# One exponential a unit, the diagonal of maxima on GpSimd, outputs turned behind the scores, and ten unread matmuls in slots without expert tiles

## The chip, the cores and the metric

The kernel runs on one core of a Trainium2 chip. The metric is the device time of one execution in microseconds, median of the runs shown.

## What is computed

A decoder layer on 64 sequences of 64 tokens with 128 channels, in float32: causal self-attention with 16 heads of 8 channels, attention to a context of the same size, and a mixture of eight experts of which each token takes two, with a layer norm behind each.

```
a = softmax(q k / sqrt(8));  o = (a v) wo + bo            # twice: causal, then to ctx
x = layernorm(x + o) * g + b                              # after each
top2 of softmax(x rw + rb), their weights by softmax
out = sum over the two of  gelu(x w1[e] + b1[e]) w2[e] + b2[e]
x = layernorm(x + out) * g + b
```

Products whose result feeds a choice of experts are made of a high and a low float16 part of each factor, so that they keep nearly float32 accuracy.

## The kernel before

The program is written out by hand for each engine, as a list of *slots*; semaphores order the engines against each other. Four slots make a step, in which one block of 256 tokens passes self-attention and an earlier one cross-attention. A *unit* is half a block (two sequences, 128 tokens) in one of the two attentions; unit g starts in slot g, and there are 64 of them in slots 0 to 71. In slot g the engines work on different stages of several units:

- TensorE: turns the normalised attention output `o_n` of unit g-3 (`turn_o`, L1549) and the normalised row of unit g-5 (`turn_y`, L1562); makes the transposed scores of unit g-1 (`scores_T`: the diagonal of maxima first, L1513, the mask, L1518, then the products, L1525); the scores of unit g (`scores`, L1495 and L1501); where the slot has an expert tile, its first product (`up`); then `weigh` of unit g-2 (probabilities times values, L1541), `out_proj` of unit g-3 (L1557), the tile's second product (`down`, L1628), and projections.
- VectorE: low halves of projections, `norm` of unit g-4 (L1136), `maxima` of unit g (the row maxima from PSUM, L1089, then a product with a constant that puts them on diagonals, L1094, so that a matmul of ones subtracts them in the transposed scores), `probs_low` of unit g-1 for ten heads (L1082), the reciprocals and `o_n` of unit g-2 (L1103, L1108), residual and statistics of unit g-3 (L1122 to L1127), and routing.
- ScalarE: copies of turned outputs, then for unit g-1 two exponentials of the same 1024 columns of PSUM, `probT` in float32 (L889) and its high part `p_hi` in float16 (L892), then copies and Gelu for tiles, and high halves.
- GpSimd: `gain` of unit g-4 (L750, L756), scatters of rows to experts and gathers of their results (in some slots), `probs_low` of unit g-1 for the other six heads (L776), `spread` of unit g-3 (variance to inverse deviation, L762, L764), `x2_low` (L770).

`weigh` waits for both low parts. `scores_T` waits for the diagonal. `norm` waits for `spread`.

Slots 0 to 32 have no expert tile. Slots 33 to 76 have one or two, the rest of the tiles and the last block (through all experts) follow as a tail. In slots 8 to 15 ScalarE and VectorE also split one expert's first weights into halves (VectorE's part is L1352). Banks of PSUM are named by their use: the diagonal goes into two banks KEYS, expert results into bank H_B.

Of the kernel before, what the change touches and what calls it, by code (L numbers as in the profile page):

```python
# [6 lines left out]
B, S, D, H, FF, E = 64, 64, 128, 16, 512, 8  # L7
# [16 lines left out]
W1_SLOT = 8  # L24
CLEAR_SLOT, CLEAR_EVERY = 10, 2
DVE_HEADS = 10
# [198 lines left out]
def tiles_in(slot):  # L225
    return [Tile(m) for m in range(NMOE) if TILE_SLOT[m] == slot]

# [83 lines left out]
def build(nc, x, ctx_in, cst, w, out):  # L311
# [17 lines left out]
    with st:  # L329
# [162 lines left out]
        lo_first, lo_second = two("probs_lo_first_heads"), two("probs_lo_second_heads")  # L492
# [217 lines left out]
        def _(pool):  # L710
# [61 lines left out]
            def probs_low(u):  # L772

                pool.wait_ge(exp_done[u.kind], u.count())
                h = slice(DVE_HEADS, H)
                pool.tensor_tensor(p_lo[u.buf][:, h, :], probT[u.buf][:, h, :], p_hi[u.buf][:, h, :], ALU.subtract).then_inc(  # L776
                    lo_second[u.kind], 1)
# [43 lines left out]
            def slot(g):  # L821
# [15 lines left out]
                if u := unit_at(g - 1):  # L837
                    probs_low(u)
# [14 lines left out]
        def _(act):  # L853
# [29 lines left out]
            def exps(u, v):  # L883
# [3 lines left out]
                if v:  # L887
# [3 lines left out]
                               scale=float(HD) ** -0.5)  # L891
                act.activation(p_hi[u.buf][:, :, :].rearrange("p h q -> p (h q)"),  # L892
                               bank[:, KEYS:KEYS + 2, :].rearrange("p a n -> p (a n)"), ACT.Exp,
# [9 lines left out]
            def y_turned(u):  # L903
# [9 lines left out]
                if b.back(1).exists():  # L913
                    act.wait_ge(lg_ready, Unit(CROSS, b.back(1), u.pair).count())
                act.activation(x2_tile[u.buf][:, :], turned_y, ACT.Identity,
                               bias=ln_bc[a][:, :], scale=ln_gc[a][:, :]).then_inc(yT_done[a], 1)

# [52 lines left out]
            def slot(g):  # L970
# [14 lines left out]
                if u := unit_at(g - 5):  # L985
                    act.wait_ge(yT_ready[u.kind], u.count())
                if u := unit_at(g - 3):
                    o_turned(u, same_buffers(g - 3))
                if u := unit_at(g - 5):
                    y_turned(u)  # L990
                if (c := chunk_closes(g)) is not None:
                    copy_y(Tile(FIRST_TILE[c] + TILES_OF[c] - 1))
                if u := unit_at(g - 1):
                    exps(u, same_buffers(g - 1))
                for x in tiles[:1]:
                    tile_step(x)
# [46 lines left out]
        def _(dve):  # L1043
# [34 lines left out]
            def probs_low(u):  # L1078
# [712 lines left out]
```

## Time and profile before

| | us |
|---|---|
| median of 3 runs | 798.61 (795.01 to 799.62) |
| the profiled execution | 803.89 |
| its span, first to last instruction | 802.1 |
| busy: TensorE, VectorE, ScalarE, GpSimd | 596.7, 488.9, 453.3, 370.1 |
| mean granted share of TensorE's clock | 0.876 |

Busy times don't say what bounds a stage: each engine is idle in some of them. A granted share of 1 is 2.4 GHz, a share of 0.5 is 1.2 GHz; what lies between is a mean over both levels.

### The profile page before, as it was taken

The numbers are of one execution on the slowest core, as the hardware profiler recorded it, in microseconds if no ns is written. First come the engines' busy times: TensorE is split into PE (matmuls) and PEld (weight loads), VectorE is DVE, ScalarE is ACT, GpSimd is POOL, SyncE is SP. The second block draws the span as 40 slices with busy tenths as digits, with TensorE's granted clock in tenths as the row PEclk, the third lists the DMA queues.
The fourth block names the chain that finished last, engine by engine and source line by source line (L and its number), as shares of the span: only waits on it lengthen the run. The fifth ranks groups of instructions, "written<-read, shape, count | busy, mean of one in ns | idle before, by whom it ended". The sixth has DMA issues, their size and how long they took to land. (4 is left out here: it accounts for less than half of the span.)

```text
span 802.1 us, 21265 instructions
## 1 busy us (share of the span) xinstructions
PE 596.7 (74%) x7870; PEld 471.7 (59%) x7870; DVE 488.9 (61%) x1337; ACT 453.3 (57%) x824; POOL 370.1 (46%) x576
## 2 busy tenths in 40 slices
PE   2776676776767698887987988698777776878970
PEld 1344444545444476765766776476666666777870
DVE  3465879767696877888776578866334651221153
ACT  1223545444333589977997889688467554334320
POOL 7122243433337544435753665387237476530350
PEclk9965878877757999998999999899989888899995
DMA  4351554843132645544655675546546457778730
GB/s 111 106 174 54 161 170 128 287 125 87 34 93 66 198 146 168 164 130 139 195 155 177 185 205 171 151 140 174 162 142 191 141 176 222 234 239 266 234 96 20
DMA packets 141413, 124.64 MB, mean 155 GB/s; under 512 B 12224, under 2 KB 123600, under 8 KB 141312
## 3 DMA queue, kind: packets, MB, share of 16 engines
q1 hardware_dynamic: 134496, 113.06, 46.6%
q0 software_dynamic: 4368, 9.05, 4.1%
q8 instruction: 64, 1.05, 0.5%
q10 hardware_dynamic: 2448, 1.18, 0.5%
q14 instruction: 37, 0.30, 0.1%
HBM read 86.81 MB, written 38.54 MB: 156 GB/s over the span
## 5 line engine op out<-in xcount | busy, mean ns | idle before, releaser
L1089 DVE TENSOR_REDUCE row_max<-bank 128x16 bf16<-128x1024 f32 x64 | 78.3, 1224 | 79.4 <-PE bank L1501 78.6
L776 POOL TENSOR_TENSOR prob_lo<-probT,prob_hi 128x384 f16<-128x384 f32 x64 | 68.7, 1073 | 92.8 <-ACT prob_hi L892 92.4
L1549 PE MATMUL bank<-consts,o_n 128*128 128x64 f32 x256 | 47.7, 316 | 81.2 <-DVE o_n L1108 71.6
L1628 PE MATMUL bank<-w_in,w_hl 128*128 128x128 f32 x704 | 106.3, 298 | 0.0
L1549 PEld LDWEIGHTS bank<-consts,o_n 128*128 128x128 f32 x256 | 39.3, 220 | 95.3 <-issue 71.0
L1628 PEld LDWEIGHTS bank<-w_in,w_hl 128*128 128x128 f32 x704 | 93.8, 207 | 0.4
L889 ACT ACTIVATE probT<-bank 128x1024 f32<-128x1024 f32 x64 | 65.6, 1024 | 46.2 <-PE bank L1525 45.8
L762 POOL TENSOR_TENSOR veps<-mv,eps 128x1 f32<-128x1 f32 x64 | 14.5, 226 | 140.3 <-DVE mv L1127 140.3
L799 POOL DMA_INDIRECT w_hl<-ys,pos x60 | 59.6, 994 | 40.5 <-DMA ys<-w_hl 23.5
L1614 PE MATMUL bank<-xT,w_in 128*128 128x128 f16 x1056 | 77.9, 226 | 0.0
L1082 DVE TENSOR_TENSOR prob_lo<-probT,prob_hi 128x640 f16<-128x640 f32 x64 | 62.3, 973 | 24.9 <-ACT prob_hi L892 24.8
L933 ACT ACTIVATE w_hl<-bank 128x512 f32<-128x512 f32 x88 | 52.6, 597 | 39.3 <-PE bank L1614 38.8
L785 POOL DMA_INDIRECT xs<-x_hl,pos x60 | 62.2, 1036 | 17.8 <-issue 17.8
L1614 PEld LDWEIGHTS bank<-xT,w_in 128*128 128x128 f16 x1056 | 67.0, 102 | 0.0
L1525 PEld LDWEIGHTS bank<-q_st,k_all 128*64 128x64 f16 x2048 | 44.5, 126 | 36.4 <-issue 36.4
L892 ACT ACTIVATE prob_hi<-bank 128x1024 f16<-128x1024 f32 x64 | 65.1, 1018 | 0.0
L901 ACT ACTIVATE oT<-bank 128x128 f32<-128x128 f32 x64 | 17.7, 277 | 75.9 <-PE bank L1562 61.4
L750 POOL TENSOR_TENSOR yg<-yn,ln_g 128x128 f32<-128x128 f32 x64 | 29.5, 460 | 66.3 <-DVE yn L1136 66.3
L1094 DVE TENSOR_TENSOR max_diag<-consts_bf,row_max 128x1024 bf16<-128x1024 bf16 x64 | 53.4, 834 | 2.2
L1513 PE MATMUL bank<-max_diag,consts_bf 128*128 128x512 bf16 x128 | 47.8, 460 | 7.5 <-DVE max_diag L1094 7.5
L933 ACT ACT_TABLE_LOAD x41 | 52.6, 1283 | 0.7
L1525 PE MATMUL bank<-q_st,k_all 128*64 128x64 f16 x2048 | 52.1, 212 | 0.0
(173 smaller groups left out, 1556.8 us busy)
## 6 DMA issues: line engine op xcount, KB each, us to landing
w_in<-w_scr SPq DMA_DIRECT2D x96, 512.0 KB, 3.7
q_scr<-q_hl SPq DMA_DIRECT2D x64, 128.0 KB
k_scr<-k_hl SPq DMA_DIRECT2D x64, 128.0 KB, 2.3
q_st<-q_scr SPq DMA_DIRECT2D x32, 256.0 KB, 3.9
k_all<-k_scr SPq DMA_DIRECT2D x128, 64.0 KB, 2.1
xs_tile<-xs SPq DMA_DIRECT2D x42, 128.0 KB
ys<-w_hl SPq DMA_DIRECT2D x42, 128.0 KB, 2.1
xs<-xs_tile SPq DMA_DIRECT2D x3, 1472.0 KB, 6.8
```

Of the source, the lines that this page charges most:

```text
L776: pool.tensor_tensor(p_lo[u.buf][:, h, :], probT[u.buf][:, h, :], p_hi[u.buf][:, h, :], ALU.subtract).then_inc(lo_second[u.kind], 1)
L785: pool.indirect_dma_start(xs[c], bass.IndirectOffsetOnAxis(pos[c][:, k, t:t + 1], 0), x2_hl[:, n, :], None).then_inc(scattered[c], 16)
L799: pool.indirect_dma_start(got[f % 2][:, t, k, :], None, ys[c], bass.IndirectOffsetOnAxis(pos[c][:, k, n:n + 1], 0)).then_inc(got_in[f % 2] ...
L889: act.activation(probT[u.buf][:, :, :].rearrange("p h q -> p (h q)"), bank[:, KEYS:KEYS + 2, :].rearrange("p a n -> p (a n)"), ACT.Exp, sc ...
L892: act.activation(p_hi[u.buf][:, :, :].rearrange("p h q -> p (h q)"), bank[:, KEYS:KEYS + 2, :].rearrange("p a n -> p (a n)"), ACT.Exp, sca ...
L933: act.activation(hid[x.par][:, :, :].rearrange("p c t -> p (c t)"), expert_h(x), ACT.Gelu, scale=1 / W1_SCALE).then_inc(h_done, 1)
L1082: dve.tensor_tensor(p_lo[u.buf][:, h, :], probT[u.buf][:, h, :], p_hi[u.buf][:, h, :], ALU.subtract).then_inc(lo_first[u.kind], 1)
L1089: dve.reduce_max(row_max[u.buf][:, :], bank[:, SC:SC + 2, :].rearrange("p a (h k) -> p (a h) k", k=S), AX.X).then_inc(max_done[a], 1)
L1525: last = pe.matmul(bank[64 * h:64 * h + 64, KEYS + n, 64 * hh:64 * hh + 64], k[:, gg, j, c:c + 64], q[:, gg, c:c + 64], start=False, stop= ...
L1549: last = pe.matmul(turned_o[:, 64 * b:64 * b + 64], o_n[u.buf][:, b, :, :, :].rearrange("p c a d -> p (c a d)"), consts[:, C_DELTA:C_TRI], ...
L1614: last = pe.matmul(v[:, c * P:(c + 1) * P], w1_t[x.wb][:, i, c * P:(c + 1) * P], xT[x.par][:, j * P:(j + 1) * P], start=False, stop=True, ...
L1628: last = pe.matmul(expert_y(x), hid[x.par][:, c, :], w2_t[x.wb][:, c, :], start=False, stop=c == FC - 1, skip_group_check=True)
```

## The change

1. *One exponential.* ScalarE makes `probT` alone. VectorE casts it to `p_hi` and subtracts for all 16 heads, in two instructions; GpSimd's share of the subtraction goes.
2. *The diagonal on GpSimd.* The product of maxima and constant, 1024 bfloat16 elements a partition, moves from VectorE to GpSimd, behind `gain` and ahead of the slot's scatters and gathers.
3. *Outputs turned behind the scores.* In slots up to 32, which have no tile, TensorE's `turn_o` and `turn_y` come after `scores_T` and `scores`, and ScalarE's copies of them after the exponential. Slots with a tile keep their order.
4. *Unread matmuls.* In slots 0 to 32 TensorE makes two times five matmuls of 512 columns from constants into bank H_B, which nothing reads there.

(`probs_low` stands twice in the old program; the first piece with it is GpSimd's, the second VectorE's. The last piece is TensorE's slot.)

```diff
+KEEP_BUSY = 5
-DVE_HEADS = 10
+def turns_late(slot):
+    return not tiles_in(slot) and chunk_closes(slot) is None and slot < ATTENTION_END
...
-            def probs_low(u):
-                pool.wait_ge(exp_done[u.kind], u.count())
-                h = slice(DVE_HEADS, H)
-                pool.tensor_tensor(p_lo[u.buf][:, h, :], probT[u.buf][:, h, :], p_hi[u.buf][:, h, :], ALU.subtract).then_inc(
-                    lo_second[u.kind], 1)
+            def spread_maxima(u):
+                pool.wait_ge(max_done[u.kind], u.count())
+                m = row_max[u.buf][:, :].rearrange("p (a c) -> p a c", c=2).unsqueeze(2).to_broadcast([P, HP, S, 2])
+                dl = neg_delta.rearrange("p (q c) -> p q c", c=2).unsqueeze(1).to_broadcast([P, HP, S, 2])
+                pool.tensor_tensor(max_diag[u.buf][:, :, :, :], dl, m, ALU.mult).then_inc(diag_ready[u.kind], 1)
...
                 if u := unit_at(g - 4):
                     gain(u)
+                if u := unit_at(g):
+                    spread_maxima(u)
                 for c, n, k in scatters_at(g):
                     scatter(c, n, k)
...
-                act.activation(p_hi[u.buf][:, :, :].rearrange("p h q -> p (h q)"),
-                               bank[:, KEYS:KEYS + 2, :].rearrange("p a n -> p (a n)"), ACT.Exp,
-                               scale=float(HD) ** -0.5).then_inc(exp_done[a], 1)
...
+            def probs_low(u, v):
                 dve.wait_ge(exp_done[u.kind], u.count())
-                h = slice(0, DVE_HEADS)
-                dve.tensor_tensor(p_lo[u.buf][:, h, :], probT[u.buf][:, h, :], p_hi[u.buf][:, h, :], ALU.subtract).then_inc(
-                    lo_first[u.kind], 1)
+                if v:
+                    dve.wait_ge(pv_ready[v.kind], v.count())
+                dve.tensor_copy(p_hi[u.buf][:, :, :], probT[u.buf][:, :, :]).then_inc(hi_done[u.kind], 1)
+                dve.wait_ge(hi_done[u.kind], u.count())
+                dve.tensor_tensor(p_lo[u.buf][:, :, :], probT[u.buf][:, :, :], p_hi[u.buf][:, :, :], ALU.subtract).then_inc(
+                    lo_done[u.kind], 1)
...
+            def keep_busy(g):
+                if 0 <= g < ATTENTION_END and not tiles_in(g):
+                    for _ in range(KEEP_BUSY):
+                        pe.matmul(bank[:, H_B, :], ones_bf, cbf[:, 0:512], start=True, stop=True, skip_group_check=True)
...
-                u, v = unit_at(g - 3), unit_at(g - 5)
-                if u or v:
-                    turn_free()
...
+                if not turns_late(g):
+                    turn_both(g)
                 if u := unit_at(g - 1):
                     scores_T(g, u)
                 if u := unit_at(g):
                     scores(g, u)
+                if turns_late(g):
+                    turn_both(g)
                 for x in tiles[:1]:
                     up(x)
+                keep_busy(g)
...
                     weigh(u)
                 if u := unit_at(g - 3):
                     out_proj(u)
+                keep_busy(g)
```

The next rows are from VectorE's list, from `norm` of one unit to `o_n` of another, before the change.

```order
L1136 TENSOR_SCALAR yn<-res,mv,rstd 128x128
L1089 TENSOR_REDUCE row_max<-bank 128x16
L1094 TENSOR_TENSOR max_diag<-consts_bf,row_max 128x1024
L1082 TENSOR_TENSOR prob_lo<-probT,prob_hi 128x640
L1103 RECIPROCAL rden<-bank 64x16 x2
L1108 TENSOR_TENSOR o_n<-bank,rden 64x8x2x8 x2
```

The same stretch of VectorE's list after it.

```order
L1143 TENSOR_SCALAR yn<-res,mv,rstd 128x128
L1100 TENSOR_REDUCE row_max<-bank 128x16
L1091 CAST prob_hi<-probT 128x1024
L1093 TENSOR_TENSOR prob_lo<-probT,prob_hi 128x1024
L1110 RECIPROCAL rden<-bank 64x16 x2
L1115 TENSOR_TENSOR o_n<-bank,rden 64x8x2x8 x2
```

The diagonal has gone from behind the maximum, and a cast and a subtraction of all 1024 elements stand there. On GpSimd, the rows of one slot before were these.

```order
L750 TENSOR_TENSOR yg<-yn,ln_g 128x128
L756 TENSOR_TENSOR x_rows<-yg,b_bo 128x128
L776 TENSOR_TENSOR prob_lo<-probT,prob_hi 128x384
L762 TENSOR_TENSOR veps<-mv,eps 128x1
L764 TENSOR_TENSOR rstd<-veps,minus_half 128x1
```

And these are GpSimd's rows of such a slot now.

```order
L755 TENSOR_TENSOR yg<-yn,ln_g 128x128
L761 TENSOR_TENSOR x_rows<-yg,b_bo 128x128
L782 TENSOR_TENSOR max_diag<-consts_bf,row_max 128x1024
L767 TENSOR_TENSOR veps<-mv,eps 128x1
L769 TENSOR_TENSOR rstd<-veps,minus_half 128x1
```

The place of the subtraction is taken by the diagonal. TensorE's list, in a slot without a tile, had the turning first.

```order
L1549 MATMUL bank<-consts,o_n 128x64 x2
L1562 MATMUL bank<-consts,yn 128x128
L1513 MATMUL bank<-max_diag,consts_bf 128x512 x2
L1518 MATMUL bank<-consts_bf 128x512 x2
L1525 MATMUL bank<-q_st,k_all 64x64 x32
L1501 MATMUL bank<-k_all,q_st 64x256 x8
```

Now TensorE's list has it behind the scores, with five unread matmuls (L1653) after it.

```order
L1520 MATMUL bank<-max_diag,consts_bf 128x512 x2
L1525 MATMUL bank<-consts_bf 128x512 x2
L1532 MATMUL bank<-q_st,k_all 64x64 x32
L1502 MATMUL bank<-consts_bf 128x512 x2
L1508 MATMUL bank<-k_all,q_st 64x256 x8
L1555 MATMUL bank<-consts,o_n 128x64 x2
L1568 MATMUL bank<-consts,yn 128x128
L1653 MATMUL bank<-consts_bf 128x512 x5
```

The wait for `o_n` no longer stands ahead of the scores there.

## Rows read from the trace of the kernel before

**Rows 1.** Windows, of the maximum (L1089) alone: its busy time and count, granted clock, DMA
```profile
75.00:203.50 128.50, 19.58 (x16) 0.79 0.51 153
203.50:283.00 79.50, 11.02 (x9) 0.78 0.34 100
283.00:443.00 160.00, 23.27 (x19) 0.96 0.55 161
443.00:570.00 127.00, 14.66 (x12) 0.97 0.57 168
```

**Rows 2.** Waits from 75 to 283 us: total, times, longest
```profile
PE bank L1549 <- DVE o_n L1108: 54.1, 23, 3.3
...
DVE row_max L1089 <- PE bank L1501: 35.1, 18, 3.9
```

**Rows 3.** Windows, all engines: PE, PEld, DVE, ACT, POOL busy (count), clock, DMA
```profile
75.00:203.50 128.50, 91.59 (x1224) 62.13 (x1226) 97.74 (x221) 59.58 (x112) 44.85 (x81) 0.79 0.51 153
...
283.00:443.00 160.00, 137.94 (x2105) 109.87 (x2104) 122.16 (x317) 138.82 (x235) 79.96 (x128) 0.96 0.55 161
```

**Rows 4.** Timeline of a slot with a tile: start, length, instruction, idle before
```profile
315.37 1.23 DVE L1089 TENSOR_REDUCE row_max<-bank 128x16 bf16<-128x1024 f32 x1 [1.53 <-PE bank L1501]
...
316.63 0.69 DVE L1094 TENSOR_TENSOR max_diag<-consts_bf,row_max 128x1024 bf16<-128x1024 bf16 x1
...
316.72 1.38 POOL L776 TENSOR_TENSOR prob_lo<-probT,prob_hi 128x384 f16<-128x384 f32 x1 [1.81 <-ACT prob_hi L892]
...
317.24 1.54 DVE L1082 TENSOR_TENSOR prob_lo<-probT,prob_hi 128x640 f16<-128x640 f32 x1
...
319.25 0.59 DVE L1108 TENSOR_TENSOR o_n<-bank,rden 64x128 f32<-64x128 f32 x2
...
319.99 0.63 PE L1549 MATMUL bank<-consts,o_n 128*128 128x64 f32 x4 [0.76 <-DVE o_n L1108]
...
320.57 0.61 PE L1513 MATMUL bank<-max_diag,consts_bf 128*128 128x512 bf16 x2
...
321.02 0.59 PE L1518 MATMUL bank<-consts_bf 128*128 128x512 bf16 x2
...
322.02 0.73 POOL L743 TENSOR_TENSOR x_bo<-tok_in,bo 128x256 f32<-128x256 f32 x1
...
322.07 0.61 PE L1501 MATMUL bank<-k_all,q_st 128*64 128x256 f16 x8
...
322.72 1.23 DVE L1089 TENSOR_REDUCE row_max<-bank 128x16 bf16<-128x1024 f32 x1 [0.58 <-PE bank L1501]
...
324.68 0.82 DVE L1082 TENSOR_TENSOR prob_lo<-probT,prob_hi 128x640 f16<-128x640 f32 x1
```

**Rows 5.** Timeline of VectorE, a slot without tiles
```profile
152.74 1.23 DVE L1089 TENSOR_REDUCE row_max<-bank 128x16 bf16<-128x1024 f32 x1 [0.57 <-PE bank L1501]
...
154.61 1.53 DVE L1082 TENSOR_TENSOR prob_lo<-probT,prob_hi 128x640 f16<-128x640 f32 x1
156.07 0.51 DVE L1103 RECIPROCAL rden<-bank 64x16 f32<-64x16 f32 x2
...
159.68 1.23 DVE L1089 TENSOR_REDUCE row_max<-bank 128x16 bf16<-128x1024 f32 x1
```

**Rows 6.** Timeline, GpSimd ahead of VectorE
```profile
224.56 0.91 POOL L776 TENSOR_TENSOR prob_lo<-probT,prob_hi 128x384 f16<-128x384 f32 x1
224.71 1.32 DVE L1094 TENSOR_TENSOR max_diag<-consts_bf,row_max 128x1024 bf16<-128x1024 bf16 x1
```

**Rows 7.** Groups of instructions: second exponential, smallest subtraction on GpSimd
```profile
L892 ACT ACTIVATE prob_hi<-bank 128x1024 f16<-128x1024 f32 x64 | 65.1, 1018 | 0.0
...
L770 POOL TENSOR_TENSOR x_hl<-x_rows,x_hl 128x128 f16<-128x128 f32 x32 | 13.5, 423 | 0.0
```

**Rows 8.** Groups of instructions: low part of expert weights, one scatter
```profile
L785 POOL DMA_INDIRECT xs<-x_hl,pos x60 | 62.2, 1036 | 17.8 <-issue 17.8
...
L1352 DVE SCALAR_TENSOR_TENSOR w_hl<-w_in,w_hl 128x512 f16<-128x512 f32 x8 | 5.4, 673 | 0.1
```

More of the change, by code:

```diff
@@ L491, in build @@
         v_hi_ready = two("v_hi_ready")
-        lo_first, lo_second = two("probs_lo_first_heads"), two("probs_lo_second_heads")
+        hi_done, lo_done = two("probs_hi"), two("probs_lo")
         lg_ready, lg_done, route = sem("lg_ready"), sem("lg_done"), sem("route_step")
@@ L836, in slot @@
                     last_spread(f)
-                if u := unit_at(g - 1):
-                    probs_low(u)
                 if u := unit_at(g - 3):
@@ L890, in exps @@
                                bank[:, KEYS:KEYS + 2, :].rearrange("p a n -> p (a n)"), ACT.Exp,
-                               scale=float(HD) ** -0.5)
-                act.activation(p_hi[u.buf][:, :, :].rearrange("p h q -> p (h q)"),
-                               bank[:, KEYS:KEYS + 2, :].rearrange("p a n -> p (a n)"), ACT.Exp,
                                scale=float(HD) ** -0.5).then_inc(exp_done[a], 1)
@@ L916, in y_turned, with both_turned @@
                                bias=ln_bc[a][:, :], scale=ln_gc[a][:, :]).then_inc(yT_done[a], 1)
+            def both_turned(g):
+                if u := unit_at(g - 5):
+                    act.wait_ge(yT_ready[u.kind], u.count())
+                if u := unit_at(g - 3):
+                    o_turned(u, same_buffers(g - 3))
+                if u := unit_at(g - 5):
+                    y_turned(u)
             def x2_high(u):
@@ L984, in slot @@
                     act.wait_ge(late_in, 16 * LATE_WEIGHTS)
[L985 to L990, printed above, removed]
+                if not turns_late(g):
+                    both_turned(g)
                 if (c := chunk_closes(g)) is not None:
@@ L994, in slot @@
                     exps(u, same_buffers(g - 1))
+                if turns_late(g):
+                    both_turned(g)
                 for x in tiles[:1]:
@@ L1090, in maxima @@
                                bank[:, SC:SC + 2, :].rearrange("p a (h k) -> p (a h) k", k=S), AX.X).then_inc(max_done[a], 1)
-                dve.wait_ge(max_done[a], u.count())
-                m = row_max[u.buf][:, :].rearrange("p (a c) -> p a c", c=2).unsqueeze(2).to_broadcast([P, HP, S, 2])
-                dl = neg_delta.rearrange("p (q c) -> p q c", c=2).unsqueeze(1).to_broadcast([P, HP, S, 2])
-                dve.tensor_tensor(max_diag[u.buf][:, :, :, :], dl, m, ALU.mult).then_inc(diag_ready[a], 1)
             def outputs(u):
@@ L1359, in slot @@
                 if u := unit_at(g - 1):
-                    probs_low(u)
+                    probs_low(u, same_buffers(g - 1))
                 if u := unit_at(g - 2):
@@ L1532, in weigh @@
                 a, b = u.kind, u.blk
-                pe.wait_ge(lo_first[a], u.count())
-                pe.wait_ge(lo_second[a], u.count())
+                pe.wait_ge(lo_done[a], u.count())
                 pe.wait_ge(v_done[a], b.times(1, 1))
@@ L1563, in turn_y, with turn_both @@
                 turned.append((yT_done[u.kind], u.count()))
+            def turn_both(g):
+                u, v = unit_at(g - 3), unit_at(g - 5)
+                if u or v:
+                    turn_free()
+                if u:
+                    turn_o(u)
+                if v:
+                    turn_y(v)
             def logits(u):
@@ L1682, in slot @@
                     pe.wait_ge(late_in, 16 * LATE_WEIGHTS)
-                u, v = unit_at(g - 3), unit_at(g - 5)
-                if u or v:
-                    turn_free()
-                if u:
-                    turn_o(u)
-                if v:
-                    turn_y(v)
+                if not turns_late(g):
+                    turn_both(g)
                 if (c := chunk_closes(g)) is not None:
@@ L1695, in slot @@
                     scores(g, u)
+                if turns_late(g):
+                    turn_both(g)
                 for x in tiles[:1]:
```

1 line of the change is left out of this document (removed).

## The prediction

> **What bounds the kernel now.** I read first how many units of attention (one row maximum each) end in which stretch, with the granted clock, then the chain of waits, then single slots of the timeline. Of the 64 units, 25 end between 75 and 283 us, in slots without expert tiles: 16 in 128.5 us (8.03 us each), then 9 in 79.5 us (8.83). 19 end from 283 to 443 us beside one expert tile a slot (8.42), 12 from 443 to 570 us (10.6) [rows 1]; the last four end among tail tiles. What follows them (the rest of the tail, the dense experts) is not edited.
>
> In the slots without tiles the longest waits of the two engines that matter point at each other: TensorE waits 54.1 us for `o_n` before it turns it, VectorE waits 35.1 us for the scores before the maximum [rows 2]. So the period is one loop: maximum, diagonal, low part, reciprocals, `o_n` on VectorE, then turning, `scores_T`, `scores` on TensorE. TensorE is busy 91.6 of 128.5 us at a mean granted clock of 0.79, a mix of 2.4 and 1.2 GHz [rows 3].
>
> One slot with a tile shows the same loop closed: the maximum starts at 315.37, runs 1.23, the diagonal 0.69 from 316.63, the low part of ten heads ends at 318.78, `o_n` at 319.84, TensorE turns from 319.99, starts `scores_T` at 320.57, ends `scores` at 322.68, and the next maximum starts at 322.72: 7.35 us [rows 4]. VectorE alone has a loop of its own in a slot without tiles where the scores come early: from the maximum at 152.74 to the next at 159.68, 6.94 us, with 3.61 of it from the reciprocals at 156.07 on (outputs, residual, statistics, the two small powers on GpSimd, norm) [rows 5].
>
> **A lock that both loops hit.** In [rows 4] GpSimd's `prob_lo` starts at 316.72, while VectorE's diagonal runs to 317.32, and takes 1.38; VectorE's `prob_lo`, issued at 317.24, takes 1.54. Alone the two take 0.91 and 0.82 [rows 4, 6]. GpSimd got nothing until 317.32, ended 0.78 later at 318.10, and only then VectorE did its work, ending 0.68 later. The other way round in [rows 6]: GpSimd's 0.91 from 224.56 is undisturbed, and the diagonal that starts 0.15 later takes 1.32 in place of 0.69, ending 0.56 after it. So a GpSimd product and a VectorE instruction of these kinds exclude each other for a whole instruction, and the one that waits goes next. The Trainium skill (SBUF — State Buffer, "SBUF: two separate sides") calls the shared port pair "an exclusive lock, not a bandwidth split" and counts a VectorE operation in a two-port mode, a float32 copy too, among those that take it. By that rule, the trace agrees for the two-input kinds; no row here shows the copy.
>
> **The change, part by part.**
>
> *ScalarE* loses 64 exponentials of 1.02 us [rows 7]. From 283 to 443 us it is busy 138.8 of 160 us, 7.3 a unit [rows 3], so in some of those slots it is the limit, in others VectorE is, as in [rows 4]. The edit takes that limit to 6.3 and shortens nothing that VectorE closes.
>
> *VectorE* loses the diagonal (0.69 alone) and its 640 elements (0.82), and gains a cast of 1024 elements and a subtraction of 1024. The trace has no such cast: the cheapest row of its size is the 16-bit diagonal, 0.69, the dearest the maximum, 1.23 for as many elements [rows 4]. I take 0.69, since it is SBUF to SBUF with one input. For the subtraction I take the rate of the maximum, 1.23: 640 in 0.82 continues to it.
>
> *GpSimd* loses 384 elements and gains the diagonal of 1024, right behind the maximum. Its price D is the largest unknown. Rows for sums and differences: 128 elements 0.42, 256 in 0.73, 384 in 0.91 [rows 4, 6, 7]. From 128 to 384 that is 1.91 ns an element and gives 0.42 + 896 x 0.00191 = 2.13; from 128 to 256, 2.4 ns and 2.6 us. I take 2.25, nearer the first, whose rows write 16 bits too. Bounds: 0.69, if it ran as on VectorE, and 3.4, eight times the row of 128. The Trainium skill (GPSIMD Engine Reference, "Elementwise — side-by-side cycle accounting") has about 2.6 cycles an element at 1.2 GHz for two inputs, which as an estimate is 2.2 us for the elements and 2.4 with a start; the sum would be some 7 us longer by it.
>
> *The order.* At the end of the maximum both the cast (VectorE, in 0.03) and the diagonal (GpSimd, semaphore about 0.1) are ready. The cast goes first and ends at 0.72. GpSimd, waiting, is next, and ends at 0.72 + D - 0.13 = 2.84 (in [rows 4] it took 0.78 of its 0.91 after it was let in). The subtraction then ends 1.23 - 0.14 = 1.09 later, at 3.93. Before, the low part ended 318.78 - 316.60 = 2.18 after the maximum in [rows 4], 2.17 in [rows 5]. So the stretch from maximum to low part grows by **1.75 us** in each unit whose loop VectorE closes. The diagonal has left VectorE's list but not its time.
>
> *Slots with a tile* keep their old order on TensorE, so the loop stays: 7.35 + 1.75 = 9.1 us.
>
> *Slots without a tile* turn outputs behind the scores, which breaks the loop through TensorE. What is left is VectorE's own, 6.94 + 1.76 = 8.7 us. TensorE's, from the maximum over the product to `scores_T` and `scores`, is 1.27 + 2.84 + 0.06 + 2.7 = 6.9, and hides. The ten matmuls cost 0.225 each at full clock (two take 0.45, 320.57 to 321.02 [rows 4]), 2.2 us; TensorE's 91.6/16 = 5.7 busy us a unit [rows 3] and these make 7.9, still under 8.7, and lift the busy share from 0.71 to 0.9. The slots with tiles, that busy, are granted 0.96 [rows 1], so I take the clock near 1. Its gain lies under VectorE's loop and is worth nothing here.
>
> *Sum.* 75 to 203 us: 16 units at 8.7, eight of them with 0.67 more for the low part of the first expert weights [rows 8], which VectorE no longer hides: 144.6 - 128.5 = +16. 203 to 283 us: three units of routing, on VectorE already, +1.75 each; four with three scatters each, 1.04 us a piece [rows 8], which now stand behind the product on GpSimd and hold the power for the next norm to about 9.4, +1; two at 8.7: together +12. 283 to 443 us: 19 units, +1.75 where VectorE closed the loop and less where ScalarE did, 1.5 on the mean: +28. 443 to 570 us: 10.6 us a unit, where a second tile or four gathers often bound: +1 each, +12. The first four and the last four units +3. Total **+71 us**. The profiled execution is 803.9 us (span 802.1), 5.3 over the median of 798.6; 798.6 + 71 gives **870 us**.
>
> **The rivals.**
> 1. *GpSimd's product costs much less, or VectorE's work goes beside it* (ends faster). If the exclusion does not hold for the cast and the 16-bit product, or the subtraction gets in first, the low part ends 1.9 after the maximum, the product at 3.9, and `scores_T` starts at once: slots with a tile 3.9 + 0.06 + 2.13 + 0.04 + 1.23 = 7.4, slots without about 7.7 by the two engines' own loops: 25 x -0.5 and 31 x -0.1, **about 783 us**. The same if D is 0.7. For it: nothing in the rows, but no row has this product. Against: [rows 4, 6]. It decides below D = 2.25 - 71/60, about 1.1 us. Chance 0.09.
> 2. *Break even*, D near 1.1 or half of the stalls hidden where ScalarE bound: within 4 us of **799 us**. Chance 0.05.
> 3. *The clock stays low in the slots without tiles*, so that the unread matmuls are in the way: twice 0.225 each at 1.2 GHz, 4.5 a slot, beside 5.7 x 0.79/0.5 = 9.0 of the rest, 13.5 us against 8.7: 25 x 4.8 more, **990 us**. Against: the busy share rises. Chance 0.02.
> 4. *D near its upper bound*, 3.4 (the broadcast operands read slowly): 60 x 1.15 = 69 more, **939 us**. Chance 0.05.
> 5. The forecast, D between 1.9 and 2.7: 60 units x 0.35 or 0.45 either way is 849 to 897. Chance 0.79.
>
> **How the numbers follow.** The range takes the forecast's own bounds, some 11 us below for the stretches costed by a mean, and above them the part of rival 4 up to D = 3.0: 838 to 915. Outside stay rivals 1 to 3 and the rest of 4, 0.19. A difference under 0.5% (4 us) can't be told from none by this kernel's runs. Faster: rival 1 and a part of 2, 0.10. Same 0.04. Slower 0.86.
>
> **What would show it.** The diagonal on GpSimd lasting 2.8 or so when it waits behind the cast and 2.1 to 2.4 alone; VectorE's full subtraction at about 3 us in place of 1.2; VectorE busy (stalled) most of each slot from 75 to 283 us; the wait of TensorE for `o_n` gone there, but grown in slots with tiles; the granted clock near 1 from 75 us on; ScalarE some 64 us less busy; 25 units in about 236 us, 19 in about 188. It is wrong if the product lasts about 1 us, if the subtraction runs undisturbed beside it, or if the exponential comes so late that GpSimd's product is done before the cast wants to start.

## The result and the profile after

The changed kernel takes 866.17 us (median of 4 runs, 864.23 to 868.99) against 799.0 (795.01 to 799.62) for the kernel before on the same chip: a ratio of 1.0855, 95% interval 1.0808 to 1.0902. The profiled execution took 865.69 us, its span 863.9. The forecast was 870. What is said of single stretches comes from one profiled execution of each kernel, and these lie up to 9 us beside the median of their runs.

The page of the changed kernel, its span and busy times:

```profile
span 863.9 us, 21892 instructions
...
PE 655.3 (76%) x8200; PEld 496.7 (57%) x8200; DVE 585.6 (68%) x1337; ACT 400.0 (46%) x760; POOL 462.2 (54%) x576
```

ScalarE is 53 us less busy, not the 64 or so of the forecast: the exponential that went had overlapped its neighbours by about 0.1 us at either end. GpSimd is 92 us more busy, as moved work would make it. VectorE is 97 us *more* busy, although it lost a product and gained only a cast and 384 more elements a unit. Where that comes from, the groups of instructions of the page say (busy time and mean ns of one, then the idle time before them), and below them each line's shortest/median/longest duration in ns:

```profile
L782 POOL TENSOR_TENSOR max_diag<-consts_bf,row_max 128x1024 bf16<-128x1024 bf16 x64 | 144.0, 2249 | 74.3 <-DVE row_max L1100 72.5
...
L1093 DVE TENSOR_TENSOR prob_lo<-probT,prob_hi 128x1024 f16<-128x1024 f32 x64 | 164.1, 2563 | 2.2
...
L1091 DVE CAST prob_hi<-probT 128x1024 f16<-128x1024 f32 x64 | 46.0, 719 | 9.4 <-ACT probT L894 9.3
```

```profile
L782 POOL TENSOR_TENSOR max_diag<-consts_bf,row_max x64: 1892/2272/2873, 29.2 to 681.5; 128x1024 bf16<-128x1024 bf16 x64
L1093 DVE TENSOR_TENSOR prob_lo<-probT,prob_hi x64: 1224/2799/2801, 36.0 to 686.9; 128x1024 f16<-128x1024 f32 x64
L1091 DVE CAST prob_hi<-probT x64: 676/683/2302, 35.2 to 686.2; 128x1024 f16<-128x1024 f32 x64
```

A subtraction that can take 1.22 us takes 2.80 in 54 of 64 units. In the other ten it runs before the product or without one, and takes 1.2 to 1.4. Two slots of the timeline show why. First VectorE and GpSimd of the changed kernel in a slot without a tile (start, duration, engine):

```profile
149.66 1.21 DVE L1100 TENSOR_REDUCE row_max<-bank 128x16 bf16<-128x1024 f32 x1
150.79 0.68 DVE L1091 CAST prob_hi<-probT 128x1024 f16<-128x1024 f32 x1
...
151.51 2.80 DVE L1093 TENSOR_TENSOR prob_lo<-probT,prob_hi 128x1024 f16<-128x1024 f32 x1
154.23 0.51 DVE L1110 RECIPROCAL rden<-bank 64x16 f32<-64x16 f32 x2
...
157.69 1.23 DVE L1100 TENSOR_REDUCE row_max<-bank 128x16 bf16<-128x1024 f32 x1
```

```profile
150.95 2.27 POOL L782 TENSOR_TENSOR max_diag<-consts_bf,row_max 128x1024 bf16<-128x1024 bf16 x1
```

The product starts at 150.95, during the cast, which ends at 151.47; it ends at 153.22. The subtraction, issued at 151.51, ends at 154.31, 1.09 after the product. That is the order of the forecast: cast, product, subtraction, one at a time. And a slot with a tile, with TensorE's rows:

```profile
338.18 1.23 DVE L1100 TENSOR_REDUCE row_max<-bank 128x16 bf16<-128x1024 f32 x1 [2.60 <-PE bank L1508]
...
339.32 0.68 DVE L1091 CAST prob_hi<-probT 128x1024 f16<-128x1024 f32 x1
...
339.49 2.27 POOL L782 TENSOR_TENSOR max_diag<-consts_bf,row_max 128x1024 bf16<-128x1024 bf16 x1 [2.84 <-DVE row_max L1100]
...
340.04 2.80 DVE L1093 TENSOR_TENSOR prob_lo<-probT,prob_hi 128x1024 f16<-128x1024 f32 x1
...
343.31 0.59 DVE L1115 TENSOR_TENSOR o_n<-bank,rden 64x128 f32<-64x128 f32 x2
...
344.05 0.63 PE L1555 MATMUL bank<-consts,o_n 128*128 128x64 f32 x4 [1.97 <-DVE o_n L1115]
...
345.12 1.05 PE L1525 MATMUL bank<-consts_bf 128*128 128x512 bf16 x2
346.10 1.06 PE L1532 MATMUL bank<-q_st,k_all 128*64 128x64 f16 x32
346.98 1.04 PE L1508 MATMUL bank<-k_all,q_st 128*64 128x256 f16 x8
...
348.06 1.23 DVE L1100 TENSOR_REDUCE row_max<-bank 128x16 bf16<-128x1024 f32 x1 [1.86 <-PE bank L1508]
```

The loop of [rows 4] is still there, but longer: the low part ends 3.43 us after the maximum (342.84 less 339.41) where it was 2.18, TensorE stands idle 1.97 us for `o_n`, and the next maximum comes 9.88 us after this one (348.06 less 338.18), not 7.35. One thing is new: two matmuls of 512 columns need 0.98 us (345.12 to 346.10), where two of that size took 0.45 in [rows 4]. TensorE has come out of its wait at the lower of its two clock levels, 1.2 GHz.

The windows of the maximum alone, as in [rows 1] (stretch, length, busy time and count, granted clock, DMA share, GB/s):

```profile
75.50:208.50 133.00, 19.55 (x16) 0.92 0.50 148
208.50:299.50 91.00, 10.98 (x9) 0.88 0.32 97
299.50:491.50 192.00, 23.27 (x19) 0.87 0.44 130
491.50:637.00 145.50, 14.67 (x12) 0.89 0.49 146
```

Taken from one unit's maximum to another's, over whole groups of slots, the time went here:

| slots | before, us a unit | after | difference in all | forecast |
|---|---|---|---|---|
| 8 to 23 | 8.03 | 8.30 | +4 | +16 |
| 24 to 32 | 8.86 | 10.11 | +11 | +12 |
| 33 to 51 | 8.43 | 10.11 | +32 | +28 |
| 52 to 65 (12 units) | 10.51 | 12.09 | +19 | +12 |
| the first 8 and 66 to 71 | | | +3 | +3, with the last four units |
| behind the last maximum | 191.7 | 183.7 | -8 | 0 |

The chain of waits has moved with it. Of 76 to 299 us (waited for; total, times, longest):

```profile
PE bank L1520 <- POOL max_diag L782: 24.3, 16, 3.9
```

TensorE's 54.1 us for `o_n` in [rows 2] have gone there, and it waits for GpSimd's diagonal instead. In the slots with tiles, 299 to 491 us, `o_n` is its longest wait; before, from 283 to 443 us, the same wait came to 6.5 us in 6 units:

```profile
PE bank L1555 <- DVE o_n L1115: 37.8, 17, 5.2
```

### The profile page after: what moved, and what is told of

Read it like the earlier page. It is cut to its first block, busy times and chain, and to the rows that moved or that the text cites. A ratio compares the mean times of both kernels' runs of the same rounds, so it can differ in the third digit from the quotient of the medians.

```text
span 863.9 us, 21892 instructions
## 1 busy us (share of the span) xinstructions
PE 655.3 (76%) x8200; PEld 496.7 (57%) x8200; DVE 585.6 (68%) x1337; ACT 400.0 (46%) x760; POOL 462.2 (54%) x576
## 4 chain that ended last, share of the span: by engine, by line
issue 25%; PE 22%; DVE 21%; POOL 17%; DMA 4%; ACT 2%; SPq 1%; POOLq 0%; DVEq 0%; ACTq 0%
POOL xs L790 6%; PE bank L1643 4%; DVE prob_hi L1091 3%; DVE row_max L1100 3%; PE bank L1629 2%; DVE rden L1110 2%; POOL w_hl L804 2%; POOL max_diag L782 2%; PE bank L1532 2%; PE bank L1508 2%; PE bank L1555 2%; DVE o_n L1115 1%; PE bank L1520 1%; POOL rstd L769 1%; DMA q_scr<-q_hl 1%
## 5 line engine op out<-in xcount | busy, mean ns | idle before, releaser
L782 POOL TENSOR_TENSOR max_diag<-consts_bf,row_max 128x1024 bf16<-128x1024 bf16 x64 | 144.0, 2249 | 74.3 <-DVE row_max L1100 72.5
L1093 DVE TENSOR_TENSOR prob_lo<-probT,prob_hi 128x1024 f16<-128x1024 f32 x64 | 164.1, 2563 | 2.2
L1555 PE MATMUL bank<-consts,o_n 128*128 128x64 f32 x256 | 45.1, 303 | 76.1 <-DVE o_n L1115 71.0
L1643 PE MATMUL bank<-w_in,w_hl 128*128 128x128 f32 x704 | 102.2, 291 | 0.0
L1643 PEld LDWEIGHTS bank<-w_in,w_hl 128*128 128x128 f32 x704 | 89.8, 200 | 0.5
L1555 PEld LDWEIGHTS bank<-consts,o_n 128*128 128x128 f32 x256 | 36.9, 208 | 90.3 <-issue 78.5
L1653 PE MATMUL bank<-consts_bf 128*128 128x512 bf16 x330 | 85.8, 395 | 0.0
L804 POOL DMA_INDIRECT w_hl<-ys,pos x60 | 62.2, 1037 | 41.5 <-DMA ys<-w_hl 25.0
L790 POOL DMA_INDIRECT xs<-x_hl,pos x60 | 70.0, 1167 | 16.0 <-issue 16.0
L1143 DVE TENSOR_SCALAR yn<-res,mv,rstd 128x128 f32<-128x128 f32 x64 | 25.3, 395 | 54.1 <-POOL rstd L769 53.4
L903 ACT ACTIVATE oT<-bank 128x128 f32<-128x128 f32 x64 | 17.7, 277 | 91.3 <-PE bank L1568 83.1
```

The lines of the kernel that those rows point to most:

```text
L782: pool.tensor_tensor(max_diag[u.buf][:, :, :, :], dl, m, ALU.mult).then_inc(diag_ready[u.kind], 1)
L790: pool.indirect_dma_start(xs[c], bass.IndirectOffsetOnAxis(pos[c][:, k, t:t + 1], 0), x2_hl[:, n, :], None).then_inc(scattered[c], 16)
L804: pool.indirect_dma_start(got[f % 2][:, t, k, :], None, ys[c], bass.IndirectOffsetOnAxis(pos[c][:, k, n:n + 1], 0)).then_inc(got_in[f % 2] ...
L1093: dve.tensor_tensor(p_lo[u.buf][:, :, :], probT[u.buf][:, :, :], p_hi[u.buf][:, :, :], ALU.subtract).then_inc(lo_done[u.kind], 1)
L1555: last = pe.matmul(turned_o[:, 64 * b:64 * b + 64], o_n[u.buf][:, b, :, :, :].rearrange("p c a d -> p (c a d)"), consts[:, C_DELTA:C_TRI], ...
L1643: last = pe.matmul(expert_y(x), hid[x.par][:, c, :], w2_t[x.wb][:, c, :], start=False, stop=c == FC - 1, skip_group_check=True)
```

## The experiments

"Us a unit" are, in this order, slots 8 to 23, 24 to 32, 33 to 51 and 52 to 65. Ratios are to the kernel before on the same chip, with their 95% interval. Medians of runs on different chips are set side by side below; the kernel before took 798.02, 799.58 and 798.14 us on the three chips of these runs, and 799.0 on that of the first comparison.

### Which part costs: the changed kernel with one part undone

**Part 2 undone: the diagonal back on VectorE, behind the maximum.**

```diff
-                if u := unit_at(g):
-                    spread_maxima(u)
...
+                dve.wait_ge(max_done[a], u.count())
...
+                dve.tensor_tensor(max_diag[u.buf][:, :, :, :], dl, m, ALU.mult).then_inc(diag_ready[a], 1)
```

> The changed kernel with the diagonal back on VectorE behind the maximum; one exponential, late turns and unread matmuls stay. Exclusion theory: the stretch from the end of the maximum to the end of the low part falls from 3.43 us to 0.69 + 0.68 + 1.22 = 2.6, the low part runs 1.2 us undisturbed in nearly every unit, slots with a tile fall from 9.9 to about 8, slots without from 8.3 to about 7.9 (TensorE with its ten matmuls); 795 to 805 us. Rival (the cast and the full subtraction on VectorE, or the unread matmuls, are what costs): the time stays within 15 us of 866.

Measured: 796.61 us, ratio 0.9998 (0.9962 to 1.0035); 7.85, 8.64, 8.79 and 10.80 us a unit. The whole loss is gone. VectorE's group of the subtraction, and a slot of it:

```profile
L1091 DVE TENSOR_TENSOR prob_lo<-probT,prob_hi 128x1024 f16<-128x1024 f32 x64 | 78.5, 1227 | 2.2
```

```profile
315.79 1.23 DVE L1098 TENSOR_REDUCE row_max<-bank 128x16 bf16<-128x1024 f32 x1 [0.57 <-PE bank L1510]
317.05 0.69 DVE L1103 TENSOR_TENSOR max_diag<-consts_bf,row_max 128x1024 bf16<-128x1024 bf16 x1
317.65 0.69 DVE L1089 CAST prob_hi<-probT 128x1024 f16<-128x1024 f32 x1
318.38 1.23 DVE L1091 TENSOR_TENSOR prob_lo<-probT,prob_hi 128x1024 f16<-128x1024 f32 x1
```

Three instructions on VectorE end 2.59 us after the maximum, less than the 3.43 of two of them beside GpSimd's product. So the loss hangs on where the product is made. Whether by its length (rival: `scores_T` waits for it) or by the exclusion, this run doesn't tell; the next one does.

**The exclusion taken away, the product left on GpSimd.** In place of the subtraction from `probT`, VectorE takes the maximum of the scores in PSUM and `p_hi`, an instruction of the same size. The low parts are then not those of the probabilities; TensorE makes new scores only when VectorE has done with the old.

```diff
-                dve.tensor_tensor(p_lo[u.buf][:, :, :], probT[u.buf][:, :, :], p_hi[u.buf][:, :, :], ALU.subtract).then_inc(
+                dve.tensor_tensor(p_lo[u.buf][:, :, :], bank[:, SC:SC + 2, :].rearrange("p a (h q) -> p (a h) q", q=S), p_hi[u.buf][:, :, :], ALU.max).then_inc(
                     lo_done[u.kind], 1)
...
+                if v := next((v for q in range(g - 2, g - 9, -1) if (v := unit_at(q))), None):
+                    pe.wait_ge(lo_done[v.kind], v.count())
```

> The changed kernel, but the low part is not computed: the same VectorE instruction takes the larger of the scores in PSUM and the high part, so it reads one operand from SBUF, not two; outputs are therefore not the reference's. Its size and place stay, and the scores of a later unit wait for it. Exclusion theory: it no longer waits for GpSimd's product, lasts 1.2 us in place of 2.8, and ends about 2.0 us after the maximum in place of 3.43; slots with a tile fall from 9.9 to 7.5, about 800 us in all. Rival (the length of GpSimd's product itself, on the way to the transposed scores, is what costs, whoever else runs): within 15 us of 866.

Measured: 810.59 us, ratio 1.0145 (1.0105 to 1.0185); 8.06, 8.68, 8.73, 10.75 us a unit. From the page, and then one of the two units in which GpSimd was first:

```profile
L1093 DVE TENSOR_TENSOR prob_lo<-bank,prob_hi 128x1024 f16<-128x1024 f32 x64 | 78.4, 1225 | 2.2
```

```profile
331.62 1.90 POOL L782 TENSOR_TENSOR max_diag<-consts_bf,row_max 128x1024 bf16<-128x1024 bf16 x1 [0.27 <-DVE row_max L1100]
331.64 2.42 DVE L1091 CAST prob_hi<-probT 128x1024 f16<-128x1024 f32 x1
334.10 1.22 DVE L1093 TENSOR_TENSOR prob_lo<-bank,prob_hi 128x1024 f16<-128x1024 f32 x1
```

With one operand in PSUM the instruction never waits (1225 ns on the mean, 1.22 here), the product lasts as long as before, and 56 of the 70 us between the changed kernel and the last run (866.17 less 796.61) are back. So the exclusion between product and subtraction is the cause of most of it. The edit swaps subtraction for maximum too. That this is not what lets the instruction through shows in the kernel of part 2 alone, further down: there VectorE's two subtractions of `v_lo`, with one operand in PSUM as well, run inside a product of GpSimd in 0.86 us together, 0.42 on the mean of all 64.

```profile
28.53 1.89 POOL L784 TENSOR_TENSOR max_diag<-consts_bf,row_max 128x1024 bf16<-128x1024 bf16 x1 [6.78 <-DVE row_max L1098]
28.98 0.86 DVE L1083 TENSOR_TENSOR v_lo<-bank,v_hi 64x256 f16<-64x256 f32 x2 [0.54 <-ACT v_hi L889]
```

Some 14 us remain for the product's own length ahead of `scores_T`, for the cast (shut out in 2 of 64 units), and for a path that the run shows beside them: the product stands ahead of the small powers on GpSimd, and VectorE's `norm` waits for them 55.2 us here from 76 to 578 us, against 17.7 us from 72 to 572 with the product on VectorE.

```profile
DVE yn L1143 <- POOL rstd L769: 55.2, 32, 4.5
```

```profile
DVE yn L1145 <- POOL rstd L769: 17.7, 26, 2.0
```

The timeline rows above add what no row of before could show: a cast of float32 to float16 is shut out as well, for all of GpSimd's 1.90 us. The Trainium skill (SBUF — State Buffer, "SBUF: two separate sides") counts the float32 copy among the instructions that take the lock; by that rule, this trace agrees, with 2.42 us in place of 0.68.

**Part 4 undone: no unread matmuls** (`KEEP_BUSY = 0`).

> The changed kernel with no unread matmuls, all else as changed. Exclusion theory: VectorE's loop binds the slots without tiles, so the clock there falls from 0.92 to about 0.75 and the time moves little: 866 to 880 us. Rival (the unread matmuls stand in the way): 840 to 855 us.

Measured: 874.23 us, ratio 1.0935 (1.0879 to 1.0991); 8.20, 10.04, 10.34, 12.11 us a unit. The granted clock in slots 8 to 23, 0.92 with them, is 0.77:

```profile
79.00:210.30 131.30, 19.55 (x16) 0.77 0.50 149
```

There they raise the clock and gain nothing (8.20 against 8.30). The 8 us lie elsewhere. Three of them are in the first 8 slots, which have unread matmuls too: the maximum of slot 8 starts at 79.2 us without them and at 76.3 with them, at a granted clock of 0.80 and 1.00 up to there. Four lie in slots 33 to 51 and two behind the last maximum, where the edit changes no instruction, and their cause is open.

**Part 3 undone: the outputs turned ahead of the scores everywhere** (`turns_late` returns False).

> The changed kernel with outputs turned ahead of the scores in all slots, as before. Theory: the loop through o_n closes again in the slots without tiles, 1.27 + 3.4 + 1.06 + 0.15 + 2.7 = 8.6 us at full clock and up to 10.8 at half, against 8.3 now: 25 units x 0.3 to 2.5, 875 to 925 us. Rival (VectorE's own loop binds anyway, the order is worth nothing): within 5 us of 866.

Measured: 887.66 us, ratio 1.113 (1.1079 to 1.118); 9.19, 10.78, 10.21, 12.08 us a unit. The loop through TensorE is closed again in the first two groups: 0.89 a unit over 16 and 0.67 over 9 make 20 of the 21 us.

### What the low clock beside tiles costs

**Eight more unread matmuls in each slot with a tile**, at its end, where TensorE waited for `o_n`.

```diff
+                if tiles and g < ATTENTION_END and not tiles[-1].tail:
+                    pe.wait_ge(h_done, tiles[-1].m + 1)
+                    for _ in range(8):
+                        pe.matmul(bank[:, H_B, :], ones_bf, cbf[:, 0:512], start=True, stop=True, skip_group_check=True)
```

> The changed kernel with eight more unread matmuls of 512 columns at the end of TensorE's part of each slot with a tile, where it waits about 2 us for o_n. Theory: part of what slots with a tile lost (9.1 to 9.9 and more, where 8.6 follows from the longer stretch on VectorE) is TensorE's clock, granted 0.87 there in place of 0.96, since it waits longer; with the wait filled the clock rises to 0.95 or more and the slots fall by about 0.9 us, 838 to 850 us. Rival (the clock is no part of it; VectorE's stretch is all): within 5 us of 866, or above it by what the matmuls take.

Measured: 860.1 us, ratio 1.0777 (1.0733 to 1.082); 8.22, 10.10, 9.81, 12.10 us a unit. Windows of the maximum, slots with one tile:

```profile
298.50:484.50 186.00, 22.94 (x19) 0.97 0.47 137
```

The clock rose from 0.87 to 0.97 as meant, and 19 units gave back 0.3 us each: 6 us, where 16 to 28 were expected. In slots 52 to 65 it rose from 0.89 to 0.96 and gave back nothing. The expectation counted each half-clock matmul of the slot. Only those on the loop can count, between `o_n` and the next maximum; that most of the others lie where TensorE waits anyway is my reading, and no run takes them apart.

### The parts alone: the kernel before with one part added

**Part 2 alone: the diagonal on GpSimd, both exponentials kept.**

```diff
+            def spread_maxima(u):
+                pool.wait_ge(max_done[u.kind], u.count())
...
+                pool.tensor_tensor(max_diag[u.buf][:, :, :, :], dl, m, ALU.mult).then_inc(diag_ready[u.kind], 1)
...
+                if u := unit_at(g):
+                    spread_maxima(u)
...
-                dve.tensor_tensor(max_diag[u.buf][:, :, :, :], dl, m, ALU.mult).then_inc(diag_ready[a], 1)
```

> The kernel before with the diagonal alone moved to GpSimd, ahead of its share of the low part; two exponentials, low part split 10 to 6 heads, old order, no unread matmuls. Exclusion theory: VectorE's 640 elements and GpSimd's 1.89 us exclude each other; where GpSimd is first the low part ends 2.65 us after the maximum in place of 1.9 to 2.2, where VectorE is first it ends at 0.9 and the diagonal at 2.6: 805 to 835 us. Rival (the diagonal on GpSimd costs only together with the cast and the full subtraction): within 5 us of 798 or below.

Measured: 817.22 us, ratio 1.0262 (1.0209 to 1.0316); 7.45, 8.64, 8.83, 11.39 us a unit. Two groups, and a collision on VectorE:

```profile
L784 POOL TENSOR_TENSOR max_diag<-consts_bf,row_max 128x1024 bf16<-128x1024 bf16 x64 | 143.3, 2240 | 76.8 <-DVE row_max L1098 75.0
...
L1091 DVE TENSOR_TENSOR prob_lo<-probT,prob_hi 128x640 f16<-128x640 f32 x64 | 68.5, 1070 | 33.4 <-ACT prob_hi L901 33.2
```

```profile
302.50 1.81 DVE L1091 TENSOR_TENSOR prob_lo<-probT,prob_hi 128x640 f16<-128x640 f32 x1 [0.84 <-ACT prob_hi L901]
...
310.28 0.82 DVE L1091 TENSOR_TENSOR prob_lo<-probT,prob_hi 128x640 f16<-128x640 f32 x1
```

The same product of 2.2 us on GpSimd costs some 20 us here (18 by the medians, 21 by the ratio, from runs that lie between 808 and 824) and 70 in the changed kernel (796.61 to 866.17). VectorE has less beside it that can be shut out (640 elements, no cast), and in 48 of 64 units it isn't: its mean is 1.07 us against 0.82 undisturbed. A second path shows here as well. The product now stands ahead of the small powers on GpSimd's list, and VectorE's `norm` waits for these 90.4 us from 79 to 581 us, where before it waited 29.4 us from 75 to 570:

```profile
DVE yn L1141 <- POOL rstd L764: 90.4, 38, 6.5
```

So this run doesn't price the exclusion alone, and how its loss divides between the two paths isn't shown. The profiled execution is the fastest of the four, 9 us under their median. In it slots 8 to 23 gain 0.6 us a unit, 9 us in all, and the slots before them lose 4 and slots 52 to 65 lose 11.

**Parts 3 and 4 on the kernel before, and part 3 alone.** `turn_both` behind the scores in slots without tiles and ScalarE's copies behind the exponentials; the first of the two also with `keep_busy`.

```diff
-                u, v = unit_at(g - 3), unit_at(g - 5)
-                if u or v:
-                    turn_free()
...
+                if not turns_late(g):
+                    turn_both(g)
                 if u := unit_at(g - 1):
                     scores_T(g, u)
                 if u := unit_at(g):
                     scores(g, u)
+                if turns_late(g):
+                    turn_both(g)
```

> The kernel before with the late turns and the unread matmuls alone (parts 3 and 4); exponentials, diagonal and low part as before. Theory: the loop through o_n is gone in the slots without tiles, but ten matmuls fill TensorE, so they stay near 7.8 us as in the run with the diagonal on VectorE, against 8.03: 788 to 796 us. Rival (these parts are worth nothing): 798.

> The kernel before with the late turns alone (part 3). Theory: VectorE's own loop of about 7 us and TensorE's 5.7 busy us a unit bind the slots without tiles, 7.3 us in place of 8.03 and 8.86, so 25 units gain 0.6 to 1.0: 775 to 785 us, if the clock does not fall. Rival (the clock falls below 0.79 when nothing fills TensorE's waits, and takes the gain back): 790 us or more.

Measured: both parts 791.13 us, ratio 0.991 (0.9877 to 0.9943), 7.85, 8.15, 8.48, 10.52 us a unit; part 3 alone **781.45 us, ratio 0.9776 (0.9743 to 0.9809)**, 7.37, 8.31, 8.44, 10.52. Windows of the maximum, part 3 alone:

```profile
71.00:189.00 118.00, 19.57 (x16) 0.85 0.56 166
189.00:263.80 74.80, 10.99 (x9) 0.82 0.39 113
263.80:424.00 160.20, 23.27 (x19) 0.96 0.54 159
```

16 units in 118.0 us, not 128.5, and 9 in 74.8, not 79.5; the slots with tiles are untouched. This is the fastest version of all. The unread matmuls on top of it cost 10 us by the medians. In the profiled executions, 5 us apart, slots 8 to 23 lose 0.48 a unit with them: TensorE is busy 107.5 of 125.5 us there, against 85.6 of 118.0 without, and the clock goes from 0.85 to 0.93. Slots 24 to 32 gain 0.16.

**Parts 1 and 3, without the diagonal on GpSimd and without unread matmuls.**

> The kernel before with one exponential (cast and full subtraction on VectorE) and the late turns in slots without tiles; diagonal on VectorE, no unread matmuls. It differs from the run with late turns alone (781) by part 1 only. Theory: the end of the low part comes 2.6 us after the maximum in place of 1.9 to 2.2, on VectorE's path, and ScalarE's relief pays in a few slots with a tile only: 786 to 796 us. Rival (ScalarE bound the slots with a tile): below 778 us.

Measured: 795.39 us, ratio 0.9981 (0.9946 to 1.0016); 7.57, 8.64, 8.82, 10.80 us a unit. One exponential less on ScalarE, paid for by a cast and 384 elements on VectorE, costs 14 us against part 3 alone by the medians, 16 by the ratios.

### Late turns in the slots with tiles too

The edit is one condition, put on three kernels: the changed one, the kernel before with part 3, and the kernel with parts 1 and 3.

```diff
-    return not tiles_in(slot) and chunk_closes(slot) is None and slot < ATTENTION_END
+    return chunk_closes(slot) is None and slot < ATTENTION_END
```

> The changed kernel with the late turns in slots with a tile too (all but those that close a chunk). Loop theory: the longer stretch on VectorE costs there because TensorE turns o_n ahead of the scores; with that order gone VectorE's own loop of 8.2 us binds, slots with a tile fall from 10.1 to 8.5 to 9, and the kernel to 820 to 845 us. Rival (the stretch itself, or the product's place ahead of the transposed scores, binds in any order): within 5 us of 866.

> The kernel before with the late turns in all slots (all but those that close a chunk), no other part of the change. Theory: ScalarE, 7.3 us busy a unit, and TensorE with the tile bind the slots with a tile in the regular ones, so they gain at most 0.5 us each on the late turns' 781: 770 to 781 us. Rival (turned copies now delay the tile's turning and Gelu on ScalarE, which binds): 785 us or more.

> One exponential with the cast and full subtraction on VectorE, the diagonal on VectorE, late turns in all slots, no unread matmuls. Theory: with the turns late in slots with a tile, VectorE's own loop of 6.94 + 0.4 = 7.3 and ScalarE's 6.3 bind less than now: 760 to 778 us, the best of all. Rival (ScalarE was no limit, and the cast only lengthens VectorE's list): no better than the same order with two exponentials.

Measured: on the changed kernel 843.85 us, ratio 1.0548 (1.0498 to 1.0598), 8.23, 9.67, 9.32, 11.84 us a unit. On the kernel before with part 3, 830.16 us, ratio 1.0399 (1.0341 to 1.0457), 7.38, 7.93, 10.00, 11.73. With parts 1 and 3, 798.96 us, ratio 0.9988 (0.9956 to 1.002), 7.55, 8.30, 8.97, 11.11.

The first gains 22 us on the changed kernel. TensorE's wait for `o_n` beside tiles is 2.5 us there, not 37.8, and with no matmul added the granted clock in slots 33 to 51 is 0.94, not 0.87. The second loses 49 us on part 3 alone, 1.56 us a unit in slots 33 to 51, where a gain was expected. The third was expected to be the best of all (760 to 778) and is 4 us slower than the same kernel with early turns beside tiles. Of the second, the longest wait of a TensorE matmul from 285 to 440 us, and the place of it:

```profile
PE bank L1612 <- ACT x_tile L920: 18.9, 7, 3.0
```

```profile
318.28 1.02 ACT L894 ACTIVATE probT<-bank 128x1024 f32<-128x1024 f32 x1
...
319.20 1.02 ACT L897 ACTIVATE prob_hi<-bank 128x1024 f16<-128x1024 f32 x1
...
320.26 0.47 ACT L920 ACTIVATE x_tile<-bank,ln_bc,ln_gc 128x128 f32<-128x128 f32 x1
...
320.88 0.37 PE L1612 MATMUL bank<-ident_f,xs_tile 128*128 128x128 f16 x2 [2.87 <-ACT x_tile L920]
```

Turned late, `y` is copied out of its bank only behind two exponentials, and the tile's own turning, next on TensorE, waits 2.87 us for that copy. In a slot without a tile nothing stands there. With parts 1 and 3, and so one exponential, the waits for `x_tile` come to 12.5 us in 270 to 430 us, and with the stretched loop of the changed kernel there is more to gain from opening it. That this balance gives the one edit both signs is my reading; no run takes the two apart.

## Why the prediction was right

The step on which it rested stands. The forecast's order (cast, then the product that waited, then the subtraction) is seen in 54 of 64 units; GpSimd's product alone lasts 1.89 us and 2.27 behind a cast; VectorE's subtraction "at about 3 us" is 2.80. Undoing part 2 alone takes the loss away (1.0855 to 0.9998), and letting the last of the three read PSUM, with the product untouched, takes 56 of 70 us away. Rival 1, in which the work goes side by side, fell with the 2.80 us of L1093, and rivals 3 and 4 with a clock of 0.92 and a product of 1.89.

Its terms were less good than their sum, and that the sum came within 4 us is in part luck:

- **D, the product's price.** Taken at 2.25 us, it is 1.89 alone, the lower edge of "D between 1.9 and 2.7": the line through rows with float32 operands, from 128 to 384 elements, was too steep for this product. From the cast's end it takes 1.75, not 2.12, and the cast ends 0.60 after the maximum, not 0.72; the subtraction's 1.09 behind it is as forecast. So the low part ends 3.43 after the maximum and a unit's stretch grows by 1.25 us, not 1.75. At 1.25 us for 19 units the slots with one tile would have lost 24 us.
- **75 to 203 us, +16.** It was +4. The period forecast was 8.7 us and 0.67 for the expert weights; the usual slot there is 8.23 (8.03 in the one shown), which is 8.7 less the 0.5 by which the stretch was overrated. The 0.67 costs nothing: the slots that have it, 8 to 15, take 8.17 on the mean, and 16 to 23 take 8.44. VectorE does that work between the statistics and the norm, where it waits for the small powers on GpSimd: in one slot it starts at 114.37, lasts 0.66, and `norm` behind it still waits 0.71 us; before the change it was 107.46, 0.66 and 0.72.
- **203 to 283 us, +12.** It was +11. The terms that are named (three times 1.75, four times 1, two at 8.7 against a mean of 8.83) make 9, so the agreement is not theirs.
- **283 to 443 us, +28.** It was +32, by other terms: 1.25 a unit make 24; the clock, which fell from 0.96 to 0.87 because TensorE now waits about 2 us for `o_n` ahead of `scores_T`, makes some 6 by the run that filled the wait; 2 are open. That TensorE's waits beside tiles took the clock down has a second witness in the changed kernel with late turns everywhere: there the wait is gone and the clock is 0.94. The forecast let the clock near 1 everywhere and didn't ask what a longer wait does to it. That an edit which fills TensorE in one place starves it in another was the missed rival.
- **443 to 570 us, +12.** It was +19, 1.58 a unit where 1 was taken; there too `o_n` comes late in more slots than the mean of [rows 1] suggested: TensorE waits for it 23.0 us in 7 units, where it waited 5.6 us in 4. VectorE's `norm` waits 21.8 us for the small powers on GpSimd, where it waited 16.5. The clock is not the cause: filling the slots with matmuls took it from 0.89 to 0.96 and left the period at 12.10. How the 7 us more than forecast divide among the rest stays open.
- **The tail, 0.** It is 8 us shorter in the profiled execution. Nothing was edited there, it lay between 183 and 192 us in the profiled executions of the other kernels (183 to 189 with the product on GpSimd, 187 to 192 with it on VectorE), and its cause is open.

The errors cancel: 12 us too many in the first stretch and 8 in the tail against 11 too few beside tiles, so the span grew by 61.8, with 71 forecast. The median grew by 67 because the profiled execution of before lay 5 us over its median and that of the changed kernel did not: that, too, brings the forecast nearer to the result than its terms are. That the clock's gain from the unread matmuls "is worth nothing here" was right for slots 8 to 32 (8.20 without them, 8.30 with, in slots 8 to 23), as was the wait of TensorE for `o_n` gone there and grown beside tiles. "The granted clock near 1 from 75 us on" was wrong: 0.92, then 0.87 to 0.89.

The parts, priced by these runs: part 3 alone takes 18 us off the kernel before; part 1 on top of it adds 14 to 16; part 4 adds 10 on part 3 alone, nothing measurable with part 1 beside it (795.39 to 796.61), and takes 8 off the whole change; part 2 adds some 20 alone and 70 on top of the others.

## What to carry to other kernels

Price an operation that moves to GpSimd by what VectorE runs at that moment, not by VectorE's list: here a 0.69 us product left VectorE and made one of its instructions 1.6 us longer in 54 of 64 units, and where VectorE's neighbour reads PSUM, or comes later, the same product costs about a quarter (14 and some 20 us in place of 70). Ask as well what stands behind it on GpSimd's own list: in both of those cases VectorE's wait for the small powers behind the product grew (55 and 90 us, against 18 and 29 with the product on VectorE). Try the parts of a joint change apart, the pure re-ordering first: it was worth 18 us, and three further parts turned that into a loss of 67. And before an engine is filled to lift its clock, look whether its list has room in that stage, and which of its matmuls lie on the path: a clock of 0.97 in place of 0.87 returned 6 us, and where the list was nearly full, the filling cost 10.

## What the runs showed of the hardware

- The exclusion takes whole instructions in turn, and a waiting engine is let in between two neighbouring instructions of the other: GpSimd's product entered between cast and subtraction, which stand 0.04 us apart on VectorE's list (151.47 to 151.51), in 54 of 64 units.
- A VectorE instruction with one operand in PSUM, of the same size and output, runs through GpSimd's product: 1.22 us where the one with both in SBUF took 2.80. The first was a maximum and the second a subtraction; a smaller subtraction with one operand in PSUM (64 x 256, 0.42 us) ran through the product too.
- A product of 1024 bfloat16 elements on GpSimd takes 1.89 us (2.27 when it has waited behind the cast), and 1.75 from the cast's end at 151.47 to its own at 153.22, so about 0.14 of it seems to be done while it waits. On VectorE the same product is 0.69.
- The cast of 1024 float32 elements to float16 on VectorE is 0.68 us, little over half of the subtraction's 1.22 for as many.
- TensorE's granted clock fell and rose with its waits: with about 2 us of waiting for `o_n` in each slot beside tiles, 0.87; with eight unread matmuls in that place, 0.97; with the wait gone by late turns, 0.94; without the ten unread matmuls, 0.77 in slots 8 to 23 in place of 0.92.
